# Queries and keys projected once per batch and copied into the row stacks by transfers of GpSimd

## The chip, the cores and the metric

The kernel runs on one core of a Trainium2 chip. Its engines are TensorE (PE in the profile; PEld is its weight load), VectorE (DVE), ScalarE (ACT), GpSimd (POOL) and SyncE (SP), beside 16 DMA engines. The metric is the device time of one execution in microseconds, as the median of several runs.

## The reference

The input is x of 16 batches, 512 rows, 128 columns, in f32. A layer norm gives xn, and the output is x plus an attention branch plus a feed-forward branch, both taken from xn:

```python
def attention(x, ...):                      # 16 heads of 8 columns
    xn = layernorm(x) * ln_g + ln_b
    q, k, v = xn @ Wq + bq, xn @ Wk + bk, xn @ Wv + bv
    p = pe @ Wp                              # sinusoidal positions
    content = einsum('bihd,bjhd->bhij', q + u_bias, k)
    pos = relative_shift(einsum('bihd,jhd->bhij', q + v_bias, p))
    attn = softmax((content + pos) * dh ** -0.5)
    return (attn @ v) @ Wo + bo

def feed_forward(x, ...):                    # weights are +1 or -1
    h = concatenate([x, -x])
    h = relu(s0 * h @ w0) * 2
    h = relu(s1 * h @ w1) * 2
    return s2 * h @ w2
```

`relative_shift` pads the 512x512 position scores of a head by a zero column and reads them back one element per row further on.

## The kernel before

**Units and halves.** A unit is one head of one batch: 256 units. The work runs in half steps ("halves"), two per unit and 32 per batch. In each half TensorE does, in this order: two position products and two content products of 128 query rows by 512 (lines 680, 690), eight 128x128 transposes of finished scores (line 699), one entry of a job table, and sixteen small products of transposed probabilities with values (line 713). The parts of a unit lie in different halves: its positions in halves 2u to 2u+3, its content scores twelve halves later, its transposes from half 2u+17.

**The way of the scores.** ScalarE copies the position scores of a half from PSUM into `pos_sb` (line 441). SyncE writes a unit's scores, 1026 KB, to a buffer `shift` in memory (line 285), and ScalarE's queue reads them back shifted by one element per row, 1024 KB, into `sc_sb` (line 428), issued in half 2u+8. VectorE then adds the content scores and takes the row minimum (line 574), subtracts it (line 582), and after the transposes ScalarE applies the exponential (line 451). So every unit moves 2050 KB, beside 256 KB of x and 256 KB of output per batch.

**Stacks.** For precision, queries, keys and positions are kept as a coarse part (f32r) and the remainder. A stack holds four heads, each in 32 partitions; of these, 26 rows are in use (`ROWS`): rows 0 to 7, 8 to 15 and 16 to 23 hold the eight columns of a head three times, and rows 24 and 25 carry the terms of the biases u and v. To bring them there, the weights themselves are laid out in this way (`stack_w`, loaded at the start), so that one projection of 128x512 in f32 makes one stack of one batch: the jobs `QG` (line 600) and `KG` (line 605), four groups of each per batch. ScalarE evicts each to `act_sb` with a bias (line 412), and GpSimd makes the stack in two operations of 128x512 (lines 338 and 339), in which a column `LOW_Q` or `LOW_K` of zeros and ones picks the rows that hold the remainder.

**Jobs.** The table (`EARLY` and `FRONT`, `MIDDLE`, `BACK` and `END`, lines 172 to 180) says in which half of which batch TensorE does which job: transposes of normalized rows (T1, TZ), the projections, the feed-forward layers L0, L1 and L2, values V, the outputs (TO, TH, WO, TY). It has 32 entries per batch, an L1 or L2 counting twice, so each of a batch's 32 halves has one. Most jobs are evicted by ScalarE and split by GpSimd (lines 347 and 348); jobs share three buffers in `act_sb` (`N_ACT`). GpSimd also computes the scales of the layer norm (lines 309 to 314) and the normalized rows (line 248), in the order of the halves.

**Start.** `EARLY` holds the first projections and the four position projections `PG`. The first query stack is made by VectorE (lines 488 and 489); until then no position product (line 680) can start. GpSimd sets three small tiles by memsets (lines 302 to 304) ahead of the first scales.

Of the kernel before, what the change touches and what calls it, by code (L numbers as in the profile page):

```python
# [5 lines left out]
ALU = mybir.AluOpType  # L6
# [8 lines left out]
ROWS = 26  # L15


def attention_mlp(nc, x, consts, stack_w, wp, pe_t, k0, k1, k2, out):
# [26 lines left out]
    with ExitStack() as ctx:  # L45
# [20 lines left out]
        w_sb = {n: const(D) for n in ("v", "o")}
        bias_q = const(GROUPS)
        bk_rows = const(GROUPS * DH).rearrange("p (g d) -> p g d", d=DH)
        uk_rows = const(GROUPS * DH).rearrange("p (g d) -> p g d", d=DH)
# [3 lines left out]
        stack_w_sb = sb("stack_w_sb", [P, 2, GROUPS * P])  # L73
        wq, wk = stack_w_sb[:, 0, :], stack_w_sb[:, 1, :]
        bias_k = sb("bias_k", [P, GROUPS])
        biased = sb("biased", [P, H, DH])
        by_bias = sb("by_bias", [P, 2, H])
        bk_uk = sb("bk_uk", [P, GROUPS, DH])
# [18 lines left out]
        KS = sb("k_stack", [P, GROUPS, S], F32R)  # L97
        PS = sb("p_stack", [P, GROUPS, S], F32R)
# [9 lines left out]
        o_t = sb("o_t", [P, S])  # L108
        wp_sb, pe_sb = o_t, heads[:, :, :, :].rearrange("p t h d -> p (t h d)")
# [7 lines left out]
        h2 = sb("h2", [P, C2, 2, S], F32R)  # L117
        y_t = sb("y_t", [P, S])
# [24 lines left out]
        s_qs, s_ks, s_ps = sem("s_qs"), sem("s_ks"), sem("s_ps")  # L143
# [28 lines left out]
        EARLY = ((-32, "TZ", 0), (-31, "PG", 0), (-30, "QG", 0), (0, "KG", 0), (1, "PG", 1), (1, "T1", 0),  # L172
                 (2, "QG", 1), (4, "PG", 2), (4, "L0", 0), (5, "L0", 1), (6, "KG", 1), (7, "PG", 3), (7, "L0", 2),
                 (8, "V", 0), (9, "QG", 2), (10, "KG", 2), (11, "L0", 3))
# [9 lines left out]
        STATS, NORM_X, NORM_Z = -50, -41, -27  # L184
# [12 lines left out]
        def job(name, b, c=0):  # L197
# [3 lines left out]
        BANK = {("TZ", 0, 0): ps_pt[:, 0, :], ("QG", 0, 0): ps_pt[:, 1, :], ("PG", 0, 0): ps_con[:, 0, :],  # L201
                ("PG", 0, 1): ps_con[:, 1, :], ("PG", 0, 2): ps_con[:, 0, :], ("PG", 0, 3): ps_con[:, 1, :],
                ("KG", 0, 0): ps_pt[:, 0, :]}
        RAW = {("QG", 0, 0): sc_sb[:, 4, 0, :], ("KG", 0, 0): sc_sb[:, 4, 1, :], ("PG", 0, 0): sc_sb[:, 5, 0, :],
               ("PG", 0, 1): sc_sb[:, 5, 1, :], ("PG", 0, 2): sc_sb[:, 5, 2, :], ("PG", 0, 3): sc_sb[:, 5, 3, :]}

        SPLITS = ("T1", "L0", "L1", "QG", "KG")
# [51 lines left out]
        def _(sp):  # L259
# [6 lines left out]
            sp.dma_start(stack_w_sb[:, :, :].rearrange("p a c -> p (a c)"), stack_w).then_inc(s_w, 16)  # L266
# [27 lines left out]
        def _(pool):  # L294
# [9 lines left out]
            pool.memset(v_sb[:, :, :, :, DH:DH + 1], 1.0).then_inc(s_ones, 1)  # L304

# [16 lines left out]
            def stack(dst, src, low, ready):  # L322
                own(pool.tensor_tensor(dst, src, low.broadcast_to([P, S]), ALU.mult))
                own(pool.tensor_tensor(dst, src, dst.bitcast(F32), ALU.subtract))
                pool.sem_inc(ready, 1)

            def split(name, b, c):
# [3 lines left out]
                if name in ("QG", "KG"):  # L331
                    dst, low, ready = {"QG": (QS, LOW_Q, s_qs), "KG": (KS, LOW_K, s_ks)}[name]
                    dst = dst[:, c, :]
                    if b == 0 and c == 1 and name == "QG":
                        pool.wait_ge(s_qs, 1)
                    if b > 0:
                        pool.wait_ge(s_con, scored(content_end(H * (b - 1) + GROUP * (c + 1) - 1), 2 * CONTENT_LAG))
                    own(pool.tensor_tensor(dst, src, low.broadcast_to([P, S]), ALU.mult))  # L338
                    pool.tensor_tensor(dst, src, dst.bitcast(F32), ALU.subtract).then_inc(s_hl, 1)  # L339
# [10 lines left out]

            scales(0)
            pool.wait_ge(s_c, 16)
            for h in HALVES:
                for name, b, c in taken(h):
                    if (name, b, c) == ("KG", 0, 0):
                        pool.wait_ge(s_jev, job("KG", 0))
                        stack(KS[:, 0, :], RAW[("KG", 0, 0)], LOW_K, s_ks)
                    elif (name, b, c) in ACTS:
                        split(name, b, c)
                if h == 5:  # L360
                    scales(1)
# [445 lines left out]
```

## Time and profile before

| | us |
|---|---|
| median of 3 runs | 1471.57 |
| range of the runs | 1469.15 to 1471.65 |
| the profiled execution | 1474.37 |
| its span in the profile | 1472.5 |

Busy times in the profiled execution: TensorE 1445.2 us (98%), VectorE 1332.8 us (91%), ScalarE 1228.7 us (83%), GpSimd 730.7 us (50%). The DMAs moved 550.40 MB at a mean of 374 GB/s.

How to read it: a busy share is an average over the whole span, and matmuls are pipelined with modelled ends, so times of single matmuls overlap. What a step costs TensorE is read from the start of one group to the start of the next. "DMA share" is the mean share of time in which the 16 DMA engines had a packet under way; it can lie a little above 1 where packets overlap. The windows and timelines count from the start of the span.

### The profile page before, as it was taken

The numbers are of one execution on the slowest core, as the hardware profiler recorded it, in microseconds if no ns is written. First come the engines' busy times: TensorE is split into PE (matmuls) and PEld (weight loads), VectorE is DVE, ScalarE is ACT, GpSimd is POOL, SyncE is SP. The second block draws the span as 40 slices with busy tenths as digits, with TensorE's granted clock in tenths as the row PEclk, the third lists the DMA queues.
The fourth block names the chain that finished last, engine by engine and source line by source line (L and its number), as shares of the span: only waits on it lengthen the run. The fifth ranks groups of instructions, "written<-read, shape, count | busy, mean of one in ns | idle before, by whom it ended". The sixth has DMA issues, their size and how long they took to land.

```text
span 1472.5 us, 41301 instructions
## 1 busy us (share of the span) xinstructions
PE 1445.2 (98%) x16040; PEld 955.1 (65%) x16040; DVE 1332.8 (91%) x3483; ACT 1228.7 (83%) x1368; POOL 730.7 (50%) x725
## 2 busy tenths in 40 slices
PE   6999999999999999999999999999999999999997
PEld 2466666666666666766666666666766666666664
DVE  4789999999989999999999999999999999989995
ACT  4588888888888888888888888888888888888873
POOL 4646555554554556455554555455455554534400
PEclk7699999999999999999999999999999999999998
DMA  3999999999999999999999999999999999999991
GB/s 131 346 377 401 384 392 397 385 399 374 402 390 372 403 384 401 376 399 392 380 402 383 391 389 392 392 382 396 386 394 392 382 406 376 401 377 390 393 402 41
DMA packets 80434, 550.40 MB, mean 374 GB/s; under 512 B 9328, under 2 KB 10096, under 8 KB 14704
## 3 DMA queue, kind: packets, MB, share of 16 engines
q1 hardware_dynamic: 42944, 278.35, 49.0%
q10 hardware_dynamic: 37296, 269.41, 47.4%
q8 instruction: 128, 2.10, 0.6%
q14 instruction: 66, 0.54, 0.1%
HBM read 274.57 MB, written 273.15 MB: 372 GB/s over the span
## 4 chain that ended last, share of the span: by engine, by line
PE 96%; ACT 2%; DVE 1%; DMA 0%; issue 0%; ACTq 0%; DVEq 0%
PE ps_pt L699 36%; PE ps_av L713 19%; PE ps_pos L680 14%; PE ps_job L641 12%; PE ps_job L605 4%; PE ps_job L600 4%; PE ps_job L620 2%; ACT pt_sb L451 1%; PE ps_job L616 1%; PE ps_job L611 1%; PE ps_job L628 1%; PE ps_con L690 1%; PE ps_con L608 1%; PE ps_job L624 1%; PE ps_job L622 0%; DMA heads<-in_pe_t 0%
## 5 line engine op out<-in xcount | busy, mean ns | idle before, releaser
L574 DVE CUSTOM_DVE_ANT_0 sc_sb<-ps_con,sc_sb 128x512 f32<-128x512 f32 x1024 | 663.0, 684 | 91.8 <-PE ps_con L690 90.5
L441 ACT COPY pos_sb<-ps_pos 128x1024 f32<-128x1024 f32 x510 | 518.4, 1017 | 184.5 <-PE ps_pos L680 183.8
L582 DVE TENSOR_SCALAR sc_sb<-sc_sb,nmax 128x512 f32<-128x512 f32 x1024 | 604.9, 623 | 0.1
L699 PE MATMUL ps_pt<-c_sb,sc_sb 128*128 128x128 f32 x4096 | 560.6, 280 | 3.9 <-ACT pt_sb L451 2.6
L451 ACT ACTIVATE pt_sb<-ps_pt 128x1024 f32<-128x1024 f32 x512 | 525.7, 1027 | 25.2 <-PE ps_pt L699 25.1
L699 PEld LDWEIGHTS ps_pt<-c_sb,sc_sb 128*128 128x128 f32 x4096 | 439.7, 141 | 130.5 <-issue 93.4
L713 PE MATMUL ps_av<-pt_sb,v_sb 128*9 128x128 f32 x8192 | 319.9, 274 | 0.6 <-ACT pt_sb L451 0.6
L713 PEld LDWEIGHTS ps_av<-pt_sb,v_sb 128*9 128x9 f32 x8192 | 172.8, 90 | 208.4 <-issue 205.7
L347 POOL CAST h<-act_sb 128x512 fp32r<-128x512 f32 x128 | 81.8, 639 | 397.3 <-ACT act_sb L417 397.0
L680 PE MATMUL ps_pos<-p_stack,q_stack 26*128 26x512 f32 x1024 | 262.5, 502 | 3.5 <-DVE q_stack L489 2.2
L690 PE MATMUL ps_con<-k_stack,q_stack 26*128 26x512 f32 x1024 | 262.1, 497 | 2.1 <-DVE nmax L574 2.0
L641 PE MATMUL ps_job<-h,w 128*128 128x512 f32 x640 | 190.6, 420 | 0.1
L680 PEld LDWEIGHTS ps_pos<-p_stack,q_stack 26*128 26x128 f32 x1024 | 98.1, 183 | 125.7 <-issue 115.6
L348 POOL TENSOR_TENSOR h<-act_sb,h 128x512 fp32r<-128x512 f32 x128 | 165.8, 1295 | 10.4
L338 POOL TENSOR_TENSOR k_stack<-act_sb,c_sb 128x512 fp32r<-128x512 f32 x63 | 71.1, 1129 | 115.9 <-ACT act_sb L412 115.7
L338 POOL TENSOR_TENSOR q_stack<-act_sb,c_sb 128x512 fp32r<-128x512 f32 x63 | 70.8, 1124 | 115.6 <-ACT act_sb L412 114.9
L641 PEld LDWEIGHTS ps_job<-h,w 128*128 128x128 f32 x640 | 109.7, 192 | 15.5 <-ACT act_sb L417 0.6
L690 PEld LDWEIGHTS ps_con<-k_stack,q_stack 26*128 26x128 f32 x1024 | 98.5, 182 | 6.5 <-DVE nmax L574 4.6
L417 ACT ACTIVATE act_sb<-ps_job,col 128x512 f32<-128x512 f32 x128 | 87.7, 685 | 1.5 <-PE ps_job L641 1.5
L339 POOL TENSOR_TENSOR q_stack<-act_sb,q_stack 128x512 fp32r<-128x512 f32 x63 | 80.7, 1281 | 4.9
L339 POOL TENSOR_TENSOR k_stack<-act_sb,k_stack 128x512 fp32r<-128x512 f32 x63 | 80.7, 1281 | 4.9
L574 DVE DVE_READ_ACCUMULATOR2_ANT nmax<- 128x1 f32 x1024 | 83.1, 81 | 0.0
(88 smaller groups left out, 941.3 us busy)
## 6 DMA issues: line engine op xcount, KB each, us to landing
shift<-pos_sb SPq DMA_DIRECT2D x256, 1026.0 KB, 9.0
sc_sb<-shift ACTq DMA_DIRECT2D x256, 1024.0 KB, 9.4
x_sb<-in_x SPq DMA_DIRECT2D x16, 256.0 KB, 11.0
out<-x_sb SPq DMA_DIRECT2D x16, 256.0 KB, 11.2
stack_w_sb<-in_stack_w SPq DMA_DIRECT2D x1, 512.0 KB, 5.1
c_sb<-in_consts ACTq DMA_DIRECT2D x1, 422.0 KB, 3.5
o_t<-in_wp ACTq DMA_DIRECT2D x1, 256.0 KB, 5.9
heads<-in_pe_t ACTq DMA_DIRECT2D x1, 256.0 KB, 6.7
```

The costliest lines, as they stand in the source:

```text
L338: own(pool.tensor_tensor(dst, src, low.broadcast_to([P, S]), ALU.mult))
L339: pool.tensor_tensor(dst, src, dst.bitcast(F32), ALU.subtract).then_inc(s_hl, 1)
L348: pool.tensor_tensor(dst[:, 1, :], src, dst[:, 0, :].bitcast(F32), ALU.subtract) \
L441: act.copy(to, ps_pos[:, :, :]).then_inc(s_pe, 1)
L451: act.activation(pt_sb[:, 2 * i:2 * i + 2, :], ps_pt[:, :, :], ACT.Exp, scale=-1.0) \
L574: dve.tensor_tensor_reduce(sc_sb[:, m % N_SC, t, :], ps_con[:, k, :], sc_sb[:, m % N_SC, t, :], -SCALE, 3.4e38, ALU.add, ALU.min, nmax[:, ...
L582: dve.tensor_scalar(sc_sb[:, m % N_SC, t, :], sc_sb[:, m % N_SC, t, :], nmax[:, m % N_SC, t:t + 1], None, ALU.subtract).then_inc(s_sub, 1)
L641: return pe.matmul(ps_job[:, :], lhs, src[:, a, hl, :], start=(a == 0 and hl == 0), stop=(a == len(before) - 1 and hl == 1))
L680: ins = pe.matmul(ps_pos[:, bank, :], QS[rows, g, t * P:(t + 1) * P], PS[rows, g, :], start=True, stop=True)
L690: pe.matmul(ps_con[:, bank, :], QS[rows, g, t * P:(t + 1) * P], KS[rows, g, :], start=True, stop=True).then_inc(s_con, 1)
L699: last = pe.transpose(ps_pt[:, j % 2, t * P:(t + 1) * P], sc_sb[:, u % N_SC, t, j * P:(j + 1) * P], id_sb)
L713: last = pe.matmul(ps_av[32 * t:32 * t + DH + 1, h % 4, :], v_sb[:, b % 2, j, h, :], pt_sb[:, j, t * P:(t + 1) * P], start=(j == 0), stop= ...
```

## The change

Queries and keys of a batch are projected once for all 16 heads, by jobs `QB` and `KB`: 128 output columns, with Wq and Wk as they are. ScalarE evicts each once, and GpSimd splits it into a coarse part and a remainder (`q_hl`, `k_hl`, 128 x 2 x 512). The stacks are then filled by transfers that GpSimd issues: a function `spread` copies, for one group of four heads, the 32 partitions of the group three times, into every fourth row of the stack from row 0, 1 and 2 (2 KB per row, 64 KB per transfer). For the queries these are coarse, coarse, remainder, for the keys coarse, remainder, coarse. That makes 24 transfers per batch: the queries of a group are issued in halves divisible by 8, eight halves before its first use, the keys in the halves after with remainder 2, ten halves before. Each group has a semaphore, and TensorE waits for 48 (three transfers of 16) per batch. GpSimd waits before each group until the content scores of that group in the batch before are done.

Row 3 of every four holds, for rows 3 and 7 of a head, the terms of the biases (`ROWS` is 32, `BIAS_ROWS` 3 and 7); the rest of the query stack is 1 and that of the key stack 0, set once by two memsets of 128x2048 on GpSimd at the start. The bias u is added to the queries (with bq), so the keys need no bias rows, and v - u takes the place of v for the positions.

The job table is laid out anew with 26 entries per batch. The stacked weights (512 KB) are no longer loaded; the constants grow by 190 columns. `o_t` now shares the memory of `z_sb`, for which GpSimd has one more wait before it normalizes z, and `wp_sb` that of `sc_sb`. The first query projection is split by VectorE, and GpSimd issues its transfers in half -8.

```diff
-ROWS = 26
+ROWS = 32
+BIAS_ROWS = (3, 7)
...
-        stack_w_sb = sb("stack_w_sb", [P, 2, GROUPS * P])
-        wq, wk = stack_w_sb[:, 0, :], stack_w_sb[:, 1, :]
...
+        q_hl = sb("q_hl", [P, 2, S], F32R)
+        k_hl = sb("k_hl", [P, 2, S], F32R)
...
-        FRONT = ((-16, "T1", 0), (-9, "TZ", 0), (-6, "V", 0), (-5, "QG", 0), (-3, "L0", 0), (-1, "KG", 0),
-                 (1, "KG", 1), (2, "QG", 1), (3, "L0", 1), (7, "L0", 2), (9, "QG", 2), (10, "KG", 2), (11, "L0", 3))
-        MIDDLE = ((12, "L1", 0, 2), (14, "KG", 3), (15, "QG", 3), (17, "L1", 1, 2), (20, "L1", 2, 2),
-                  (24, "L1", 3, 2), (36, "L2", 0, 2), (38, "TO", 0), (40, "TO", 1))
-        BACK = ((51, "TO", 2), (54, "TO", 3), (60, "TH", 0), (62, "WO", 0), (64, "TY", 0))
+        FRONT = ((-19, "T1", 0), (-18, "TZ", 0), (-11, "QB", 0), (-9, "V", 0), (-5, "L0", 0), (-3, "L0", 1),
+                 (-1, "KB", 0), (0, "L0", 2), (8, "L0", 3))
+        MIDDLE = ((9, "L1", 0, 2), (15, "L1", 1, 2), (17, "L1", 2, 2), (24, "L1", 3, 2), (33, "L2", 0, 2),
+                  (39, "TO", 0), (44, "TO", 1))
+        BACK = ((52, "TO", 2), (54, "TO", 3), (58, "TH", 0), (60, "WO", 0), (62, "TY", 0))
...
+            pool.memset(QS[:, :, :].bitcast(F32), 1.0).then_inc(s_fill, 1)
+            pool.memset(KS[:, :, :].bitcast(F32), 0.0).then_inc(s_fill, 1)
...
+                if k == 1:
+                    wait(pool, s_job, job("WO", b - 3))
...
-                if name in ("QG", "KG"):
-                    dst, low, ready = {"QG": (QS, LOW_Q, s_qs), "KG": (KS, LOW_K, s_ks)}[name]
-                    dst = dst[:, c, :]
...
-                    own(pool.tensor_tensor(dst, src, low.broadcast_to([P, S]), ALU.mult))
-                    pool.tensor_tensor(dst, src, dst.bitcast(F32), ALU.subtract).then_inc(s_hl, 1)
+                if name in ("QB", "KB"):
+                    dst, ready, landed = {"QB": (q_hl, s_qh, s_q), "KB": (k_hl, s_kh, s_k)}[name]
+                    wait(pool, landed[GROUPS - 1], 48 * b)
+                    own(pool.tensor_copy(dst[:, 0, :], src))
+                    pool.tensor_tensor(dst[:, 1, :], src, dst[:, 0, :].bitcast(F32), ALU.subtract).then_inc(s_hl, 1)
...
+            def spread(k, stack, hl, thirds, ready, landed):
+
+                b, g = divmod(k, GROUPS)
+                if not 0 <= b < B:
+                    return
+                pool.wait_ge(ready, b + 1)
+                if b > 0:
+                    pool.wait_ge(s_con, scored(content_end(H * (b - 1) + GROUP * (g + 1) - 1), 2 * CONTENT_LAG))
+                for third, part in enumerate(thirds):
+                    pool.dma_start(stack[third:P:4, g, :], hl[32 * g:32 * g + 32, part, :]).then_inc(landed[g], 16)
...
+                if h % 8 == 0:
+                    if h == -8:
+                        pool.wait_ge(s_fill, 2)
+                    spread(h // 8 + 1, QS, q_hl, (0, 0, 1), s_qh, s_q)
+                if h % 8 == 2:
+                    spread(h // 8, KS, k_hl, (0, 1, 0), s_kh, s_k)
...
-                if name == "QG":
-                    return [lambda: pe.matmul(out, wq[:, c * P:(c + 1) * P], z_q[:, :],
-                                              start=True, stop=True)]
+                if name == "QB":
+                    return [lambda: pe.matmul(out, w_sb["q"], z_q[:, :], start=True, stop=True)]
...
-                    pe.wait_ge(s_qs, GROUPS * b + g + 1)
+                    pe.wait_ge(s_q[g], 48 * (b + 1))
...
-                    pe.wait_ge(s_ks, GROUPS * b + g + 1)
+                    pe.wait_ge(s_k[g], 48 * (b + 1))
```

## Rows read from the trace of the kernel before

**Rows 1.** The page: busy engines; DMA queues (packets, MB, share); chain by engine.

```profile
PE 1445.2 (98%) x16040; PEld 955.1 (65%) x16040; DVE 1332.8 (91%) x3483; ACT 1228.7 (83%) x1368; POOL 730.7 (50%) x725
...
q1 hardware_dynamic: 42944, 278.35, 49.0%
q10 hardware_dynamic: 37296, 269.41, 47.4%
...
PE 96%; ACT 2%; DVE 1%; DMA 0%; issue 0%; ACTq 0%; DVEq 0%
```

**Rows 2.** Windows: length, busy us (instructions) per engine, PEclk, DMA share, GB/s.

```profile
105.00:700.00 595.00, 594.75 (x6783) 397.69 (x6776) 556.82 (x1460) 516.99 (x576) 318.91 (x315) 1.00 1.01 391
1405.00:1430.00 25.00, 24.32 (x305) 16.05 (x304) 23.73 (x68) 19.25 (x21) 1.90 (x2) 1.00 1.01 410
1412.00:1434.00 22.00, 21.54 (x259) 14.58 (x258) 20.34 (x58) 13.83 (x16) 0.00 (x0) 1.00 1.01 420
```

**Rows 3.** TensorE's timeline: start us, us, engine, line, operation, tiles.

```profile
617.04 1.06 PE L616 MATMUL ps_job<-c_sb,z_t 128*128 128x128 f32 x8
...
704.87 1.06 PE L616 MATMUL ps_job<-c_sb,z_t 128*128 128x128 f32 x8
...
707.77 1.02 PE L600 MATMUL ps_job<-z_q,stack_w_sb 128*128 128x512 f32 x2
708.73 0.62 PE L713 MATMUL ps_av<-pt_sb,v_sb 128*9 128x128 f32 x16
...
1418.19 0.50 PE L680 MATMUL ps_pos<-p_stack,q_stack 26*128 26x512 f32 x1
...
1420.20 0.49 PE L680 MATMUL ps_pos<-p_stack,q_stack 26*128 26x512 f32 x1
```

**Rows 4.** Waits: engine, line, releaser: total us, times, longest us.

```profile
DVE sc_sb L574 <- PE ps_con L690: 90.5, 147, 2.5
...
DVE stats L480 <- DMA x_sb<-in_x: 2.2, 1, 2.2
```

**Rows 5.** DMA: landing (page); then 2.5 to 9 us; then 25 to 36.5 us.

```profile
shift<-pos_sb SPq DMA_DIRECT2D x256, 1026.0 KB, 9.0
...
DMA packets 2043, 2.28 MB, mean 350 GB/s; under 512 B 610, under 2 KB 1360, under 8 KB 2043
...
q1 hardware_dynamic: 304, 2.23, 46.9%
...
shift<-pos_sb SPq DMA_DIRECT2D x3, 1026.0 KB, 4.7
```

**Rows 6.** Groups: engine, operation, tiles, count | busy us, mean ns | idle before.

```profile
L582 DVE TENSOR_SCALAR sc_sb<-sc_sb,nmax 128x512 f32<-128x512 f32 x1024 | 604.9, 623 | 0.1
...
L347 POOL CAST h<-act_sb 128x512 fp32r<-128x512 f32 x128 | 81.8, 639 | 397.3 <-ACT act_sb L417 397.0 <-DVE v_sb L497 0.2 <-POOL k_stack L339 0.2
...
L339 POOL TENSOR_TENSOR q_stack<-act_sb,q_stack 128x512 fp32r<-128x512 f32 x63 | 80.7, 1281 | 4.9
...
L338 POOL TENSOR_TENSOR k_stack<-act_sb,c_sb 128x512 fp32r<-128x512 f32 x63 | 71.1, 1129 | 115.9 <-ACT act_sb L412 115.7 <-POOL rstd L314 0.2
```

**Rows 7.** Timeline, VectorE and GpSimd together; then L582 from 1410 us (min/median/max ns).

```profile
710.78 1.28 POOL L339 TENSOR_TENSOR q_stack<-act_sb,q_stack 128x512 fp32r<-128x512 f32 x1
...
711.05 1.29 DVE L582 TENSOR_SCALAR sc_sb<-sc_sb,nmax 128x512 f32<-128x512 f32 x1
...
L582 DVE TENSOR_SCALAR sc_sb<-sc_sb,nmax x20: 477/482/485, 1410.3 to 1431.8; 128x512 f32<-128x512 f32 x20
```

**Rows 8.** Timeline of the start.

```profile
0.80 0.33 POOL L304 MEMSET v_sb<- 128x128 f32 x1
...
5.00 0.19 POOL L309 TENSOR_SCALAR var_eps<-mv 128x4 f32<-128x4 f32 x1 [3.88 <-DVE mv L484]
...
16.14 0.50 PE L680 MATMUL ps_pos<-p_stack,q_stack 26*128 26x512 f32 x1 [2.23 <-DVE q_stack L489]
...
31.19 2.04 PE L605 MATMUL ps_job<-z_t,stack_w_sb 128*128 128x512 f32 x2
```

More of the change, by code:

```diff
@@ L14, with attention_mlp @@
 GROUP = 4
-ROWS = 26
-def attention_mlp(nc, x, consts, stack_w, wp, pe_t, k0, k1, k2, out):
+ROWS = 32
+BIAS_ROWS = (3, 7)
+def attention_mlp(nc, x, consts, wp, pe_t, k0, k1, k2, out):
     B, S, D = x.shape
@@ L62, in attention_mlp @@
         id_sb = const(P)
-        cols = const(8)
-        G, BB, BO, S0, S1, S2, LOW_Q, LOW_K = (cols[:, i:i + 1] for i in range(8))
+        cols = const(10)
+        G, BB, BO, S0, S1, S2, BQ, BK, U, LOW_K = (cols[:, i:i + 1] for i in range(10))
         bv_row = const(D)
[L66 to L69, printed above, removed]
+        w_sb = {n: const(D) for n in ("q", "k", "v", "o")}
         u_all = const(D).rearrange("p (h d) -> p h d", d=DH)
@@ L142, in attention_mlp @@
         s_hl = sem("s_hl")
-        s_qs, s_ks, s_ps = sem("s_qs"), sem("s_ks"), sem("s_ps")
+        s_fill = sem("s_fill")
+        s_qh, s_kh = sem("s_qh"), sem("s_kh")
+        s_q = [sem(f"s_q{g}") for g in range(GROUPS)]
+        s_k = [sem(f"s_k{g}") for g in range(GROUPS)]
+        s_ps = sem("s_ps")
         s_pos, s_con = sem("s_pos"), sem("s_con")
@@ L354, in _ @@
                 for name, b, c in taken(h):
[L355 to L358, printed above, removed]
+                    if (name, b, c) in ACTS:
                         split(name, b, c)
+                if h % 8 == 0:
[4 more added lines that the diff above has]
+                    spread(h // 8, KS, k_hl, (0, 1, 0), s_kh, s_k)
                 if h == 5:
@@ L519, in _ @@
             dve.wait_ge(s_c, 16)
-            dve.wait_ge(s_w, 48)
+            dve.wait_ge(s_w, 32)
             def heads_first(w):
                 return w.rearrange("p (h r) -> p h r", r=32)
-            for i, (w, by) in enumerate(((wp_sb[:, :], v_all), (wk, u_all))):
-                own(dve.tensor_tensor(biased[:, :, :], heads_first(w)[:, :, 0:DH], by, ALU.mult))
-                own(dve.reduce_sum(by_bias[:, i, :], biased[:, :, :], axis=mybir.AxisListType.X))
-                for r in (ROWS - 2, ROWS - 1):
-                    last = dve.tensor_copy(heads_first(w)[:, :, r], by_bias[:, i, :])
-                last.then_inc(s_bias, 1)
-            own(dve.tensor_tensor(bk_uk[:, :, :], bk_rows, uk_rows, ALU.mult))
-            dve.reduce_sum(bias_k[:, :], bk_uk[:, :, :], axis=mybir.AxisListType.X).then_inc(s_bias, 1)
+            w = heads_first(wp_sb)
+            own(dve.tensor_tensor(v_all, v_all, u_all, ALU.subtract))
+            own(dve.tensor_tensor(biased[:, :, :], w[:, :, 0:4 * DH:4], v_all, ALU.mult))
+            own(dve.reduce_sum(by_bias[:, :], biased[:, :, :], axis=mybir.AxisListType.X))
+            for r in BIAS_ROWS:
+                last = dve.tensor_copy(w[:, :, r], by_bias[:, :])
+            last.then_inc(s_bias, 1)
+            dve.tensor_tensor(bias_q[:, :], BQ, U, ALU.add).then_inc(s_bias, 1)
             dve.tensor_scalar(col2[:, 0:2], cols[:, 3:5], 2.0, None, ALU.mult).then_inc(s_bias, 1)
@@ L540, in _ @@
             stack(PS[:, 0, :], RAW[("PG", 0, 0)], LOW_K, s_ps)
-            dve.wait_ge(s_jev, job("QG", 0, 0))
-            stack(QS[:, 0, :], RAW[("QG", 0, 0)], LOW_Q, s_qs)
+            dve.wait_ge(s_jev, job("QB", 0))
+            own(dve.tensor_copy(q_hl[:, 0, :], RAW[("QB", 0, 0)]))
+            dve.tensor_tensor(q_hl[:, 1, :], RAW[("QB", 0, 0)], q_hl[:, 0, :].bitcast(F32), ALU.subtract) \
+               .then_inc(s_qh, 1)
             dve.wait_ge(s_rstd, 2)
@@ L653, in do_job @@
                 if part == 0 and (name, b, c) in BANK:
-                    if name in ("QG", "PG") and c == 0:
-                        pe.wait_ge(s_w, 48)
+                    if name == "PG" and c == 0:
+                        pe.wait_ge(s_w, 32)
                     if name == "PG":
```

104 lines of the change are left out of this document (35 added, 69 removed).

## The prediction

> **What bounds the kernel now.** I read the page first: TensorE is busy for 98% of the span and makes up 96% of the chain that ended last, VectorE is at 91%, and the two large DMA queues together fill 49.0 + 47.4 = 96.4% of the 16 DMA engines [rows 1]. So TensorE looks like the bound, with a second resource that has almost nothing left. The windows say it for the steady part: from 105 to 700 us TensorE is busy 594.75 of 595 us, and the DMA share is 1.01 at 391 GB/s [rows 2]. TensorE's timeline gives the period: the job of line 616 comes once per batch, at 617.04 and at 704.87 us, so a batch takes 87.83 us [rows 3]. Who waits for whom shows that the DMAs are full but not yet late: VectorE's large wait (90.5 us) is for TensorE's content scores, and the only wait for a transfer in the list is 2.2 us for x at the start [rows 4]. But a write of 1026 KB takes 9.0 us to land in the middle of the run and 4.7 us when it runs nearly alone [rows 5]: transfers queue up behind each other.
>
> **What goes from TensorE.** Each batch has four query and four key projections of 128x512 in f32. One of them occupies TensorE from 707.77 to 708.73 us, 0.96 us [rows 3]. The change keeps one of each, so six go: 6 x 0.96 = 5.8 us per batch, 92 us in all. The job table has 32 entries per batch in 32 halves now and 26 afterwards, so six halves are left with no job. Near the end a half without one takes from 1418.19 to 1420.20, 2.01 us [rows 3], only 0.73 us less than the mean half of 87.83/32 = 2.74 us, since other engines then come last. So six jobs save between 6 x 0.73 = 4.4 and 5.8 us on the path; I take the middle, 5.2. If nothing else intervened, a batch would take 87.83 - 5.2 = 82.6 us.
>
> **VectorE and GpSimd.** VectorE is busy 556.82/595 x 87.83 = 82.2 us per batch [rows 2], so it too could only just follow. Part of this is not its own work. Its line 582 lasts 623 ns on average [rows 6], but 482 ns late in the run, where GpSimd does nothing, and 1.29 us where it lies over GpSimd's line 339 [rows 7]: 64 x 0.14 = 9 us per batch are waiting for GpSimd. GpSimd is busy 318.91/595 x 87.83 = 47.1 us per batch. The change takes eight splits of 1.129 + 1.281 us from it (-19.3) and adds two of 0.639 + 1.281 (+3.8) [rows 6], which leaves 31.6, and with it a third less collision: VectorE falls to about 79 us. Against this GpSimd now issues 24 transfers per batch. The trace has no transfer issued by GpSimd, so I bound one by its smallest and its large operations, 0.33 us [rows 8] and 1.28 us [rows 6], and take the middle, 0.8: 19 us, which brings GpSimd to 51 us and VectorE back to about 83. Nothing urgent stands behind the issues: query stacks are issued 8 halves ahead of use (8 x 2.74 = 22 us), key stacks 10, and even queued transfers land in 9.0 us [rows 5]. ScalarE loses six evictions, which lie beside other work. All of this is near 83 us per batch, still 5 us below today.
>
> The Trainium skill (SBUF — State Buffer, "SBUF: two separate sides") says that a DMA issued by GpSimd waits for its descriptors while VectorE holds the port they share. The trace shows that lock in the other direction only [rows 7]. By the page a spread could come late by about one line 582 each time; with 22 us in hand that changes no term here.
>
> **The DMA engines.** Here I see the end of the gain. A batch now moves 391 GB/s x 87.83 us = 34.3 MB. The change adds 24 copies of 32 rows of 2 KB, 1.57 MB, from SBUF to SBUF. For 82.6 us this asks for 35.9/82.6 = 434 GB/s. The best that the trace shows over 22 us is 420, over 25 us 410 [rows 2]; writes that run alone move 2.23 MB in 0.469 x 11.5 us, 413 GB/s [rows 5]. So the DMA engines become the bound whatever the other engines save. What a batch costs then is uncertain on two counts. First the rate for the large transfers: between 391 (today's, if full engines can't do better) and 420. I take 410, the rate of the longer stretch, since it also holds some of the ordinary jobs. 34.3/410 = 83.7 us. Second the price of the copies: at 420 GB/s 3.7 us; at the 350 GB/s of the setup, where all packets are small [rows 5], 4.5 us. I take 4.5, as these packets are small. Sum: 88.2 us per batch against 87.83, so +0.4 us, and over 15 periods +6 us. The ends are 34.3/420 + 3.7 = 85.4 us (-36 us in all) and 34.3/391 + 4.5 = 92.2 us (+66 us).
>
> **The start.** The first stack of queries now comes by transfer: three issues and a landing stand between the split and line 680, which starts at 16.14 us today [rows 8]. Below, 1.5 us; above, three issues of 1.28 and the 4.7 us of a lone large write, 8.5; I take 4.5, because a copy is a sixteenth of that write. Two memsets of 2048 elements now stand ahead of the scales on GpSimd. By line 304 (0.33 us for 128 elements) they cost 5.3 us each, by line 347 (0.639 us for 512) 2.6 each; GpSimd is free from 1.13 to 5.00 us [rows 8], so the delay lies between 1.2 and 6.7 us, and I take 1.5, since a memset reads nothing. Four projections leave the first twelve halves, where one lasts 2.04 us [rows 8]: between 0 and 8.2 us, and I take 4, for much of the waiting there is for evictions and splits. Setup loads 512 KB of stacked weights less and 95 KB of constants more, 1.2 us at 350 GB/s. Sum 4.5 + 1.5 - 4 - 1 = +1 us, between -7 and +14.
>
> **The sum.** Span 1472.5 + 6 + 1 = 1479.5 us. The profiled execution took 1474.37 us, 1.9 more than its span and 2.8 more than the median of the runs, 1471.57. So I expect 1479.5 + 1.9 - 2.8 = 1478.6, about 1479 us.
>
> **The rivals.**
> *The engines pace it (B).* 82.6 to 83 us per batch; 16 x 5 = 80 us less, about 1392 us. For it speaks that TensorE is the whole chain [rows 1] and no wait is for a DMA [rows 4]. It needs 434 GB/s held through, which no stretch of the trace shows. The Trainium skill (DMA: Bandwidth & Descriptors, "Specifications") gives 435 GB/s as the fabric's ceiling; by that page the rival would be just possible.
> *Memory, not the DMA engines, sets 391 GB/s (C).* Then copies that never leave SBUF slip into the engines' stretched packets and cost nothing, and a batch stays at 34.3/391 = 87.8 us: 1473 us. Against it stand 420 GB/s of almost only memory traffic late in the run [rows 2]. The Trainium skill (DMA: Bandwidth & Descriptors, "Bandwidth") says that the memory side binds such transfers at about 358 GB/s and the fabric the SBUF copies; the trace's 391 is above its figure.
> *The copies cost twice (D), the slower side.* They are read from 32 neighbouring partitions and written to rows four apart, so a copy's engine crosses partitions that other transfers are using at that moment. If each holds an engine for its reading and its writing in turn, a batch costs 83.7 + 9.0 = 92.7 us: 15 x 4.9 + 1 = +74 us, about 1546. It decides the sign as soon as a copy's packets take over 4.1/4.5 = 0.9 of what I charged, at 410 GB/s.
> *Forecast (A).* The DMA engines bound it, 85.4 to 92.2 us per batch.
>
> **Chances.** A 0.70 (faster 0.26, within 0.2% 0.10, slower 0.34: its centre lies 7 us above today and its spread is some 30), B 0.10, C 0.08 (0.06 within, 0.02 faster by a good start), D 0.12. So faster 0.38, same 0.16, slower 0.46; 0.2%, 3 us, is about what a measurement of this kernel can tell from no change. The range reaches A's lower end with the start's middle (1479 - 42) and most of the way to its upper one (1479 + 60), and leaves out B and most of D: 1436 to 1530 us.
>
> **What the profile would show.** A: a batch period near 88 us, a DMA share of 1.0 or more at 400 GB/s or above, waits of VectorE or ScalarE for shift transfers that the trace has none of now, write landings well above 9.0 us, and TensorE busy near 93%. TensorE's step: no more than two pairs of line 600/605 matmuls per batch. GpSimd: about 50 us per batch and line 582's mean between 0.55 and 0.65 us. B would show a period below 84 us at 430 GB/s. C: a share of 1 at 391 GB/s plus the copies. D: the queue of the copies taking over 6 us of 16 engines per batch. I would be wrong above all if full engines do clearly better than 420 GB/s, or if copies of 2 KB rows cost far from 4.5 us.

## The result, and the profile after

The changed kernel takes 1502.29 us (median of 4 runs, 1495.67 to 1506.52) against 1471.61 us for the kernel before in the same series (1469.15 to 1473.47): a ratio of 1.0205, 95% interval 1.0163 to 1.0248. It is 31 us slower. The profiled execution took 1495.67 us, its span is 1493.8 us, 21.3 us more than the span before.

The page of the changed kernel: busy engines, the three large queues (packets, MB, share of the 16 DMA engines' time), the chain by engine and by line.

```profile
PE 1384.0 (93%) x15848; PEld 940.0 (63%) x15848; DVE 1289.7 (86%) x3479; ACT 1169.9 (78%) x1272; POOL 683.3 (46%) x919
...
q1 hardware_dynamic: 42800, 277.83, 47.4%
q10 hardware_dynamic: 37296, 269.51, 44.5%
...
q0 software_dynamic: 18432, 25.19, 5.7%
...
PE 65%; DMA 22%; ACT 6%; issue 2%; DVE 2%; ACTq 1%; POOL 1%; POOLq 0%
```

Against [rows 1]: TensorE has lost 61 us of work and is idle 7% of the span; DMA, which had no part of the chain, now makes up 22% of it. Queue 0, which is new, holds the copies. The two large queues move the same bytes as before (within 0.1%) and take 91.9% of 1493.8 us instead of 96.4% of 1472.5 us: 1373 us instead of 1419. Packets took less time each although more was moved per microsecond. More on this at the end.

Windows of the changed kernel (length, busy us and instructions of PE, PEld, DVE, ACT and POOL, granted clock, DMA share, GB/s): the long one, and four that follow each other.

```profile
105.00:700.00 595.00, 558.14 (x6557) 383.32 (x6556) 528.36 (x1426) 481.51 (x525) 285.63 (x383) 0.99 1.02 400
726.00:737.00 11.00, 11.00 (x129) 7.39 (x128) 11.00 (x26) 9.35 (x11) 7.06 (x9) 1.00 1.01 415
737.00:748.00 11.00, 10.54 (x142) 7.06 (x140) 10.55 (x31) 10.18 (x11) 5.45 (x8) 1.00 1.04 412
748.00:759.00 11.00, 7.48 (x76) 5.63 (x73) 7.60 (x21) 5.98 (x8) 1.63 (x2) 0.88 1.02 417
759.00:770.00 11.00, 10.87 (x128) 7.67 (x126) 9.11 (x25) 8.62 (x10) 5.37 (x9) 0.97 1.01 371
```

The rate is 400 GB/s over the long window, where it was 391 [rows 2]. TensorE is not short of work evenly: it works through two windows and then stands still for 3.5 us of 11, while the DMA engines move 417 GB/s. The timeline of that stop, ScalarE and TensorE:

```profile
748.28 1.02 ACT L446 COPY pos_sb<-ps_pos 128x1024 f32<-128x1024 f32 x1
...
754.08 0.52 ACTq L433 DMA_DIRECT2D sc_sb<-shift  x1
...
754.70 1.01 ACT L446 COPY pos_sb<-ps_pos 128x1024 f32<-128x1024 f32 x1 [4.14 <-DMA shift<-pos_sb]
...
755.76 0.49 PE L682 MATMUL ps_pos<-p_stack,q_stack 32*128 32x512 f32 x1 [2.79 <-ACT pos_sb L446]
```

ScalarE waits until a write of position scores has landed. Only then can it issue the read of them (L433) and copy new scores into the buffer (L446), and only then has TensorE somewhere to put the next product. The list of waits counts such stops, with the new waits for transfers; then what transfers take to land:

```profile
DVE sc_sb L581 <- PE ps_con L692: 124.6, 162, 4.2
...
ACT pos_sb L446 <- DMA shift<-pos_sb: 80.6, 30, 4.5
...
DVE sc_sb L581 <- DMA sc_sb<-shift: 6.7, 13, 2.0
...
PE ps_pos L682 <- DMA q_stack<-q_hl: 6.1, 1, 6.1
```

```profile
shift<-pos_sb SPq DMA_DIRECT2D x256, 1026.0 KB, 11.0
sc_sb<-shift ACTq DMA_DIRECT2D x256, 1024.0 KB, 11.0
q_stack<-q_hl POOLq DMA_DIRECT2D x192, 64.0 KB, 7.5
k_stack<-k_hl POOLq DMA_DIRECT2D x192, 64.0 KB, 7.6
```

[Rows 4] had one wait for x and none for the shift; writes landed in 9.0 us [rows 5]. TensorE waits for a stack once in the whole run, for the very first.

The batch period comes from the output projection, one pair of matmuls per batch some 0.45 us apart. Its first and last start in the first 14 batches (minimum, median and maximum ns of one; first to last start), in the kernel before and then in the changed one:

```profile
L611 PE MATMUL ps_job<-o_t,c_sb x28: 592/594/595, 188.3 to 1331.2; 128*128 128x512 f32 x28
```

```profile
L616 PE MATMUL ps_job<-z_sb,c_sb x28: 592/594/595, 183.9 to 1345.9; 128*128 128x512 f32 x28
```

13 periods take 1142.4 us before and 1161.5 after: 87.9 and 89.35 us, 1.47 more. Over 15 periods that is 22.0 us, so everything else together, start and end, gave back 0.7 us. The question is therefore why a batch takes 89.4 us. (The median run takes 6.6 us longer than the profiled one; if that lies in the 15 periods, its batch takes 89.8.)

### The profile page after: what moved, and what is told of

Same layout as the page of the kernel before. It is cut to its first block, busy times and chain, and to the rows that moved or that the text cites. A ratio compares the mean times of both kernels' runs of the same rounds, so it can differ in the third digit from the quotient of the medians.

```text
span 1493.8 us, 40812 instructions
## 1 busy us (share of the span) xinstructions
PE 1384.0 (93%) x15848; PEld 940.0 (63%) x15848; DVE 1289.7 (86%) x3479; ACT 1169.9 (78%) x1272; POOL 683.3 (46%) x919
## 4 chain that ended last, share of the span: by engine, by line
PE 65%; DMA 22%; ACT 6%; issue 2%; DVE 2%; ACTq 1%; POOL 1%; POOLq 0%
PE ps_pt L701 26%; DMA shift<-pos_sb 21%; PE ps_av L715 12%; PE ps_job L646 11%; PE ps_pos L682 10%; ACT pt_sb L456 4%; ACT pos_sb L446 2%; PE ps_job L625 1%; PE ps_job L616 1%; PE ps_job L611 1%; ACTq L433 1%; PE ps_job L621 1%; PE ps_job L607 1%; DMA sc_sb<-shift 1%; DVE sc_sb L581 1%
## 5 line engine op out<-in xcount | busy, mean ns | idle before, releaser
L446 ACT COPY pos_sb<-ps_pos 128x1024 f32<-128x1024 f32 x510 | 519.0, 1018 | 241.8 <-PE ps_pos L682 155.2
L589 DVE TENSOR_SCALAR sc_sb<-sc_sb,nmax 128x512 f32<-128x512 f32 x1024 | 555.8, 575 | 0.1
L682 PE MATMUL ps_pos<-p_stack,q_stack 32*128 32x512 f32 x1024 | 263.6, 505 | 58.1 <-ACT pos_sb L446 51.5
L692 PE MATMUL ps_con<-k_stack,q_stack 32*128 32x512 f32 x1024 | 262.6, 501 | 0.0
L682 PEld LDWEIGHTS ps_pos<-p_stack,q_stack 32*128 32x128 f32 x1024 | 98.5, 185 | 180.0 <-issue 106.7
L646 PE MATMUL ps_job<-h,w 128*128 128x512 f32 x640 | 201.9, 440 | 0.0
L354 POOL DMA_DIRECT2D q_stack<-q_hl x192 | 107.5, 562 | 8.0 <-DVE q_hl L548 6.8
L354 POOL DMA_DIRECT2D k_stack<-k_hl x192 | 102.5, 536 | 4.4 <-issue 4.4
L692 PEld LDWEIGHTS ps_con<-k_stack,q_stack 32*128 32x128 f32 x1024 | 98.5, 183 | 2.7 <-issue 1.3
L574 DVE COPY o_sb<-ps_av 128x512 f32<-128x512 f32 x64 | 43.9, 686 | 28.3 <-PE ps_av L715 27.3
L646 PE MATMUL ps_job<-x_t,w 128*128 128x512 f32 x128 | 47.2, 449 | 3.8 <-DVE v_sb L502 2.6
```

Source lines behind the costliest of these rows:

```text
L354: pool.dma_start(stack[third:P:4, g, :], hl[32 * g:32 * g + 32, part, :]).then_inc(landed[g], 16)
L446: act.copy(to, ps_pos[:, :, :]).then_inc(s_pe, 1)
L589: dve.tensor_scalar(sc_sb[:, m % N_SC, t, :], sc_sb[:, m % N_SC, t, :], nmax[:, m % N_SC, t:t + 1], None, ALU.subtract).then_inc(s_sub, 1)
L646: return pe.matmul(ps_job[:, :], lhs, src[:, a, hl, :], start=(a == 0 and hl == 0), stop=(a == len(before) - 1 and hl == 1))
L682: ins = pe.matmul(ps_pos[:, bank, :], QS[rows, g, t * P:(t + 1) * P], PS[rows, g, :], start=True, stop=True)
L692: pe.matmul(ps_con[:, bank, :], QS[rows, g, t * P:(t + 1) * P], KS[rows, g, :], start=True, stop=True).then_inc(s_con, 1)
```

## The experiments

Times are medians; ratios are against the kernel before on the same chip (1471.5 to 1472.9 us).

**Which engines pace the two kernels.** Two runs, one of each kernel, leave out half of every write and every read back from the seventh head on:

```diff
-sp.dma_start(chunks(shift[u % N_SHIFT]), pos_sb[:, u % N_POS]...)
+part = 1 if u < N_SHIFT else 2
+sp.dma_start(chunks(shift[u % N_SHIFT, 0:S * PITCH // part]), pos_sb[:, u % N_POS]...[:, 0:NT * PITCH // part])
```

and the read back in the same way. On the changed kernel:

> The changed kernel with all of its copies, but from the seventh head on each position write and each read back moves only half of its bytes. Left out: half of the position scores. T1: the DMA engines fall to about half and the engines set the pace: by the prediction's step 82.6 us per batch, so about 1392 to 1400 us, with TensorE near 99%. If TensorE or VectorE had a price of the change that the prediction missed (stalls for stacks that land late, GpSimd's port), the time stays above 1420 us, and the waits name it.

Measured: 1413.75 us, ratio 0.9596 (0.9581 to 0.9610). On the kernel before:

> The kernel before, with each position write and each read back from the seventh head on halved. Left out: half of the position scores. It gives the pace of the engines of before without the DMA engines. The changed kernel so halved had a period of 83.9 us, the same in every batch. Theory T1 (before is paced by its engines, the changed kernel by its transfers): the period stays at 87.8 us and the time at 1471 us (1466 to 1474). Rival T4 (both are paced by the DMA engines, whose share reads 1.01 in both): it falls to 84 us or below, 1420 us or less.

Measured: 1471.30 us, ratio 0.9994 (0.9984 to 1.0004). The windows and the output projection of both, first the changed kernel with half the transfers, then the kernel before with half:

```profile
105.00:1300.00 1195.00, 1181.33 (x14114) 813.01 (x14106) 1126.43 (x3054) 1039.53 (x1126) 607.25 (x814) 1.00 0.72 227
...
L618 PE MATMUL ps_job<-z_sb,c_sb x28: 592/594/595, 180.0 to 1271.4; 128*128 128x512 f32 x28
```

```profile
105.00:1300.00 1195.00, 1194.79 (x13628) 798.41 (x13625) 1117.34 (x2920) 1038.42 (x1158) 636.70 (x627) 1.00 0.59 199
...
L613 PE MATMUL ps_job<-o_t,c_sb x28: 592/594/595, 186.2 to 1328.4; 128*128 128x512 f32 x28
```

The kernel before has the same period with half the transfers, (1328.4 - 0.5 - 186.2)/13 = 87.8 us: its engines pace it, and the DMA share of 1.01 that it showed [rows 2] cost it nothing that this measurement can tell (the interval allows 2.4 us). The changed kernel's engines need (1271.4 - 0.5 - 180.0)/13 = 83.9 us. That is more than the 82.6 of the prediction, and the time lies between the two that the expectation had set apart (1400 and 1420). So the change does what it says: some 57 us of 1471 less for the engines (1413.75 against 1471.30). The transfers take all of it back, and 31 us more.

**What the copies cost.** Three runs: the changed kernel without copies from batch 1 on, the same with the query copies only, and the kernel before with 24 copies per batch added to it:

```diff
-if not 0 <= b < B:
+if b != 0:                                      # no copies
+if not 0 <= b < B or (b > 0 and stack is KS):   # queries only
```

> The changed kernel, but GpSimd copies queries and keys into the stacks only for batch 0; all later batches multiply with the stacks of batch 0. Left out: the filling of the stacks from batch 1 on, so the scores of batches 1 to 15 are not the reference's. Theory T1 (the DMA engines' time is the bound, and the 24 copies per batch took 5.3 us of it): the period falls from 89.3 us to about 84 us, the whole to about 1502 - 15 x 5.3 = 1420 us (1405 to 1435), DMA share still 1.0 or near it. Rival T2 (memory alone sets the rate of the large transfers, the copies slip in free, and the time was lost elsewhere, by TensorE's clock or by later evictions): 1490 to 1500 us. Rival T3 (the copies cost more than their packets show, since they hold up the large ones): below 1400 us, the engines' own pace of about 82.6 us.

Measured: 1459.99 us, ratio 0.9902 (0.9877 to 0.9926).

> The changed kernel with the query copies in every batch and the key copies in batch 0 only: 12 copies per batch instead of 24. Left out: the filling of the key stacks from batch 1 on. T1: the saving is linear in the copies, half of that without any, so about 1460 us (1450 to 1470). T2: 1490 to 1500 us. T3: the same line with a steeper slope. A threshold (all of the gain or none of it at half the dose) would show as a time off the middle between this kernel's neighbours.

Measured: 1486.52 us, ratio 1.0084 (1.0058 to 1.0111).

> The kernel before, all of its eight projections and its arithmetic kept, with 24 copies of 64 KB per batch added by GpSimd into a scratch tile that nobody reads. T1: 34.3 MB of large transfers at about 400 GB/s take 85.8 us and the copies 5.3, so the period rises from 87.83 to about 91 us and the whole from 1471.6 to about 1520 us (1500 to 1550); the 2 us between TensorE's 87.8 and the DMA engines' own 85.8 absorb a part. T2: no change, 1472 to 1476. T3: above 1550. If the issuing on GpSimd is what costs (VectorE held off the port), line 582 and its like get longer than their mean of 623 ns here, and the DMA queues do not.

Measured: 1513.61 us, ratio 1.0258 (1.0227 to 1.0289). Here the added lines are

```diff
+for third, part in enumerate(thirds):
+    pool.dma_start(twin[third:P:4, :], stack_w_sb[32 * g:32 * g + 32, part, :]).then_inc(s_twin[j], 16)
```

24 copies cost 42 us in the changed kernel (2.8 per batch) and 41 in the kernel before (2.7); 12 cost 27. So they aren't free (T2 falls), and no run came near the times of T3, which wanted more than the packets show. But the first expectation was missed by 40 us: the run without any copies should have come to 1420 and stayed at 1460, far above the engines' 1414. Half of the explanation was wrong: the large transfers alone need more than I had thought. The second expectation, 1450 to 1470 for half of the copies, was missed with it. Nor is the price even: the first twelve copies cost 27 us and the next twelve 16. Why is open.

Is it GpSimd's issuing that costs, by holding up VectorE? In the changed kernel it isn't: VectorE's subtraction lasts 575 ns with the copies and 572 without. In the kernel before the added copies lengthen it from 623 to 639 ns, 64 x 0.016 = 1 us per batch, so there a part of the 41 us may be of this kind.

**What the large transfers need by themselves.** TensorE's work is cut down, once without the copies from batch 1 on and once with all of them. Both runs leave out the products of the low parts in the layers L0, L1 and L2, 24 matmuls per batch:

```diff
-return [lambda a=a, hl=hl: product(a, hl) for a in range(len(before)) for hl in range(2)]
+return [lambda a=a: product(a, 0) for a in range(len(before))]
```

> The changed kernel without the copies from batch 1 on (as in the run without copies, 1460 us, a period of 86.5 us), and without the products of the low parts in L0, L1 and L2. Left out: the filling of the stacks from batch 1 on, and the low halves of the split products. TensorE has 24 matmuls of 0.43 us less per batch, 10 us. It asks whether 86.5 us is what the large transfers need by themselves. Theory T1 with 397 GB/s as the most that the DMA engines can hold in this mix: 86.5 us again, 1455 to 1462. Rival T6 (they can hold 410 to 420, as the forecast had it, and 86.5 is a near tie of engines at 83.9 and transfers at 82 to 84, in which each waits for the other now and then): 83 to 84 us, 1415 to 1430.

The 10 us in this and the next expectation are too much: matmuls overlap, so their lengths don't add up. From start to start a job of four matmuls takes 1.10 us and one of two 0.65 (the changed kernel, then the one with 24 matmuls less):

```profile
737.22 1.17 PE L646 MATMUL ps_job<-h,w 128*128 128x512 f32 x4
738.32 0.63 PE L715 MATMUL ps_av<-pt_sb,v_sb 128*9 128x128 f32 x16
```

```profile
735.95 0.72 PE L646 MATMUL ps_job<-h,w 128*128 128x512 f32 x2
736.60 0.63 PE L715 MATMUL ps_av<-pt_sb,v_sb 128*9 128x128 f32 x16
```

That is 0.23 us for a matmul and some 5.5 us for a batch, of the order of the change's own step.

Without copies and low products, measured: 1443.28 us, ratio 0.9817 (0.9782 to 0.9852).

> The changed kernel with all of its copies, without the products of the low parts in L0, L1 and L2: TensorE has 24 matmuls less per batch, 10 us. Left out: the low halves of the split products. It answers the run that had neither these products nor the copies (1443 us). Theory T1 (the changed kernel is bound by its transfers, TensorE's work hardly counts): 1485 to 1500 us, and the copies cost 1492 - 1443 = 49 us or 3.3 us per batch here, where the engines are well out of the way. Rival T6 (much of the 1502 is a tie of engines and transfers, which wait for each other by turns): 1460 to 1475, and the copies' own price is 1 to 2 us per batch.

Measured: 1503.38 us, ratio 1.0219 (1.0193 to 1.0244), beside the changed kernel once more:

> The changed kernel once more, unedited, as the mark for its variants: the moved jobs gave 1506 us and the plain copies 1511, and the first measurement of the changed kernel 1502. 1498 to 1508 us; above 1508 the two edits would be no slower than it.

Measured: 1502.73 us, ratio 1.0204 (1.0181 to 1.0227). Its waits of ScalarE for writes, and those of the run with the copies and without the low products:

```profile
ACT pos_sb L446 <- DMA shift<-pos_sb: 80.5, 33, 4.5
```

```profile
ACT pos_sb L446 <- DMA shift<-pos_sb: 154.5, 95, 4.6
```

The run without copies lies between its two forecasts (1455 to 1462 and 1415 to 1430); the one with them lies 3 us above T1's range and 28 above T6's, so T6 falls. With the copies, 5.5 us less of TensorE per batch change nothing (+0.7 us in all); the time turns into waits for writes. So the changed kernel is bound by its transfers, and TensorE's work no longer counts. Without the copies the same step is worth 16.7 us in all, 1.1 per batch. My reading is that engines (83.9) and transfers are close there, and each holds up the other now and then; it rests on the medians alone, since the profiled executions of the two happen to be the fastest of one and the slowest of the other (1453.8 and 1453.1 us). With less work for the engines the 24 copies cost 1503.38 - 1443.28 = 60 us, 4.0 us per batch.

The period of the run without copies and low products is what the large transfers need by themselves, at most; then that of the changed kernel in its repeated run (span 1500.5 us):

```profile
L614 PE MATMUL ps_job<-z_sb,c_sb x28: 592/594/595, 178.9 to 1306.4; 128*128 128x512 f32 x28
```

```profile
L616 PE MATMUL ps_job<-z_sb,c_sb x28: 592/594/595, 186.2 to 1353.0; 128*128 128x512 f32 x28
```

The first is (1306.4 - 0.5 - 178.9)/13 = 86.7 us in an execution 9.8 us longer than the median, which makes 86.0 us in the median run (an estimate: 86.7 - 9.8/15). The second is (1353.0 - 0.5 - 186.2)/13 = 89.7 us, and 89.7 less the 4.0 of the copies gives 85.7. So the large transfers alone need some 86 us. Both figures are about one rate: 34.3 MB in 86 us are 399 GB/s, and 35.9 MB in 89.7 us are 400. The windows from 105 to 700 us say it directly, in this order: no copies; no copies and less TensorE; copies and less TensorE; the kernel before with the copies.

```profile
105.00:700.00 595.00, 575.39 (x6825) 394.92 (x6824) 546.15 (x1483) 500.44 (x544) 213.23 (x234) 0.99 1.01 398
```

```profile
105.00:700.00 595.00, 556.75 (x6695) 376.77 (x6693) 558.43 (x1490) 494.46 (x548) 213.14 (x235) 0.99 1.01 400
```

```profile
105.00:700.00 595.00, 538.04 (x6418) 364.37 (x6417) 538.86 (x1428) 472.99 (x525) 287.71 (x384) 0.98 1.03 401
```

```profile
105.00:700.00 595.00, 584.17 (x6579) 388.41 (x6576) 550.36 (x1411) 500.54 (x562) 393.84 (x461) 0.99 1.01 397
```

397 to 401 GB/s in these, with copies and without. Over all runs that wait for writes and in both long windows (105 to 700 and 105 to 1300 us) it is 393 to 401; the lowest are the two with 12 copies per batch, 393 to 395. A copy costs about its bytes at that rate: 1.57 MB/400 = 3.9 us per batch.

What sets this rate is open. The writes use four buffers (`N_POS`), and no run has another number of them. Two things speak against too few transfers in flight: the copies come on a queue of their own, on top of the others, and the sum doesn't rise with them; and in the run with the copies and without the low products the share stays at 0.99 or above in every stretch of 5.5 us from 704 to 880 us.

**Whether it matters how a copy is made.** One run reads the same rows that it writes, one names both sides f32:

```diff
-pool.dma_start(stack[third:P:4, g, :], hl[32 * g:32 * g + 32, part, :])
+pool.dma_start(stack[third:P:4, g, :], hl[third:P:4, part, :])
+pool.dma_start(stack[third:P:4, g, :].bitcast(F32), hl[32 * g:32 * g + 32, part, :].bitcast(F32))
```

> The changed kernel, with each copy read from the same rows that it writes (third, third + 4, ...), not from 32 neighbouring ones. Left out: the right content of the stacks. The prediction's rival D had it that a copy that crosses partitions costs twice. Theory T8 (crossing from one set of partitions to another is part of the price): the packets of the copies get shorter than 98 ns and the time falls by half of the copies' 42 us, to about 1480. Rival (a copy costs its bytes and packets, wherever its rows lie): 1498 to 1508 us and 5.7% of the engines' time.

Measured: 1503.53 us, ratio 1.0207 (1.0175 to 1.0239).

> The changed kernel, output unchanged, with both sides of the copies named f32, not float32r, in the same order on GpSimd. A copy packet of 2 KB takes 98 ns in the trace, a packet of x of the same size 84. Theory T7 (a copy between tiles of float32r is handled as a cast, and that makes its packets slower): packets fall to some 84 ns, 5.7% of the engines' time to 4.9%, and the time by 24 x 32 x 14 ns / 16 = 0.7 us per batch, 10 us. Rival: a float32r copy is a plain copy; 1498 to 1505 and 5.7% again.

Measured: 1510.99 us, ratio 1.0268 (1.0251 to 1.0285). Queue 0 (packets, MB, share) of the two, in the same order:

```profile
q0 software_dynamic: 18432, 25.19, 5.5%
```

```profile
q0 software_dynamic: 12288, 25.19, 4.7%
```

Crossing partitions costs nothing that shows (1503.5 against 1502.7 us), so T8 falls. The f32 copies take a third fewer packets for the same bytes (32 per copy instead of 48) and 4.7% of the engines' time instead of 5.5 to 5.7%, near the 4.9% of T7, and the kernel isn't faster for it; it is even 0.6% slower than the changed kernel (the intervals 1.0251 to 1.0285 and 1.0181 to 1.0227 don't touch). Why it is slower stays open. What follows is that the sum of packet times isn't the price.

**Whether the order of work costs something.**

```diff
-(33, "L2", 0, 2), (39, "TO", 0)
+(35, "L2", 0, 2), (38, "TO", 0)
```

> The changed kernel, output unchanged, with two jobs moved: L2 from halves 33 and 34 to 35 and 36, the first TO from 39 to 38. The six halves without a job are then 1, 2, 5, 7, 11 and 19 of each batch instead of 3, 4, 5, 6, 11 and 19. In the trace of the changed kernel TensorE stops for 3.5 to 4 us once per batch (748 to 759 us and 836 to 847 us), just behind the four empty halves in a row, and in the 11 us after it the DMA engines move 371 to 374 GB/s instead of 401 to 420. Theory T5 (uneven work lets the engines outrun the transfers, stop, and leave the transfers short afterwards): that costs up to (410 - 372)/410 x 11 = 1 us per batch, so the time falls by 8 to 15 us to about 1490. Rival T1 pure (the DMA engines need the same time whatever the order): 1498 to 1505, no difference over 3 us, and a stop of the same sum elsewhere.

Measured: 1506.09 us, ratio 1.0237 (1.0215 to 1.0259): no gain, T5 falls. The stops move, they don't go: ScalarE's waits for writes sum to 72.9 us instead of 80.5,

```profile
ACT pos_sb L446 <- DMA shift<-pos_sb: 72.9, 30, 4.8
```

and the window from 770 to 781 us now has 350 GB/s. The low rate behind a stop is no loss that this levelling won back: over the long windows the mean is 397 to 399, against 399 to 401 without it.

**Half of the change.** Queries projected once and copied, keys projected per group as before:

```diff
-(0, "KB", 0) ... (-1, "KB", 0)
+(0, "KG", 0), (3, "KG", 1), (11, "KG", 2), (19, "KG", 3)
```

> Half of the change, output unchanged: queries projected once and copied (12 copies per batch), keys projected per group as before, into rows four apart. T1: the transfers of the run with half of the copies (1486 us) and 2.9 us more of TensorE per batch, which lies beside them: 1486 to 1495 us, no gain over the kernel before. If the engines' pace counted for more than the transfers, 29 jobs per batch at 85.9 us would come close to it: 1475 or below. It would beat both kernels only below 1470.

Measured: 1494.61 us, ratio 1.0150 (1.0102 to 1.0198). The fourth key projection lies at half 19, behind the refilling of `z_t` for the next batch at half 14, so the keys of its group come from the wrong batch; the amount of work is the same. It is slower than the kernel before, and than the same copies without the three projections (1486.5). There is little room for any dose of this change: without a single copy, which no version can have, it ends at 1460 us, 13 us below the kernel before, and twelve copies cost twice that (27 us). Doses below twelve weren't run.

## Why the prediction was right, and where it was not

The time, 1502 against the forecast 1479, lies in the range, and the mechanism is the forecast one: the transfers become the bound and take back what the engines save. But the range is wide, 94 us with both signs in it, faster had a chance of 0.38, and of the 31 us measured only 7 were forecast: the mechanism was foreseen, the size was not. Its terms, one by one:

- **The bound of before** [rows 1 to 4]: TensorE, with the transfers full but not late. Shown by the halved transfers (87.8 us per batch and 1471.3 us again).
- **TensorE's step.** 5.2 us per batch were taken, from 4.4 to 5.8. The engines' pace fell from 87.8 to 83.9, by 3.9: below the lower bound. TensorE's work did go by 87.8 - 1181.33/1195 x 83.9 = 4.9 us; but it is then idle 1 us per batch, mostly for VectorE and ScalarE. Even so, the term doesn't reach the sum, since the transfers are later.
- **VectorE and GpSimd.** VectorE is busy 1126.43/1195 x 83.9 = 79.1 us per batch in the run with half transfers, forecast 83. GpSimd is busy 42.6 us, forecast 51: a copy's issue takes 0.54 to 0.56 us, not 0.8. VectorE's L589 lasts 575 ns (0.55 to 0.65 forecast):

```profile
L589 DVE TENSOR_SCALAR sc_sb<-sc_sb,nmax 128x512 f32<-128x512 f32 x1024 | 555.8, 575 | 0.1
...
L354 POOL DMA_DIRECT2D q_stack<-q_hl x192 | 107.5, 562 | 8.0 <-DVE q_hl L548 6.8
L354 POOL DMA_DIRECT2D k_stack<-k_hl x192 | 102.5, 536 | 4.4 <-issue 4.4
```

- **The rate of the large transfers: the term that was mis-sized.** I took 410 GB/s from a 25 us window late in the run, "the rate of the longer stretch, since it also holds some of the ordinary jobs". Over 595 us the changed kernel has 400 GB/s, and the kernels that wait for their transfers have 393 to 401: some 86 us instead of 83.7. Windows of 11 us range from 371 to 420 in one batch of the changed kernel (704 to 792 us), so a window much shorter than a batch can't give a sustained rate; and 391 of the kernel before was not a limit either, but what its engines asked for. The value lay between my two bounds, and I took it near the wrong one.
- **The copies.** 4.5 us were charged, at 350 GB/s; they cost 4.0 us where transfers bind most clearly, their bytes at 400. The charge for small packets wasn't needed. It hid a part of the miss: the two errors have opposite signs.
- **Sum.** 83.7 + 4.5 = 88.2 was forecast, and the period measured is 89.7, of which some 86 are the large transfers' and 4 the copies'. 1.5 us x 15 = 22 us, which is the miss of 23.
- **The start** was forecast at +1 us. Start and end together come to -0.7. The first position product starts 19.04 - 16.14 = 2.9 us later [rows 8], where 4.5 were charged for the first stack by transfer and 1.5 for the memsets. These took 1.9 us each, in GpSimd's idle time: the first scales wait for VectorE, not for them.

```profile
0.97 1.87 POOL L304 MEMSET q_stack<- 128x2048 f32 x1
2.78 1.81 POOL L305 MEMSET k_stack<- 128x2048 f32 x1
5.92 0.19 POOL L310 TENSOR_SCALAR var_eps<-mv 128x4 f32<-128x4 f32 x1 [1.34 <-DVE mv L489]
...
15.64 1.86 POOL L354 DMA_DIRECT2D q_stack<-q_hl  x3 [6.75 <-DVE q_hl L548]
...
19.04 0.79 PE L682 MATMUL ps_pos<-p_stack,q_stack 32*128 32x512 f32 x1 [6.08 <-DMA q_stack<-q_hl]
```

- **The rivals.** B (the engines pace it, 1392) is what halving the transfers shows, 1414; it would have needed 34.3 + 1.6 = 35.9 MB in 83.9 us, 428 GB/s held, and 401 is what holds. C (memory sets the rate, copies that stay in SBUF are free) falls: they cost their full bytes, 60 us, so transfers to memory and those inside SBUF share what limits the rate, whatever it is. D (a copy costs twice, for crossing) falls: same rows, same time.
- **In the profile**: a period near 88 (89.4 to 89.7), a share over 1 at 400 GB/s or above (1.02, 400), waits for shift transfers (80.6 us), landings well above 9.0 (11.0) and TensorE at 93% (93%) all came.

The Trainium skill (Perfetto Trace Analysis, "Identifying the Most-Contended Engine") says not to judge the DMA by the busy share of its engines, which misleads, but by the use of the memory's bandwidth. The halved run of the kernel before agrees: half the bytes, and a share of 0.59 where 1.01 stood before.
The Trainium skill (DMA: Bandwidth & Descriptors, "Bandwidth") measures 425 GB/s for one core with a 16 MB transfer; with 1 MB transfers in both directions no kernel here held more than 401 over 595 us or longer.

## What to carry to other kernels

When one engine is at 98% and the DMA engines are full, find out which of the two is binding before taking work from the engine: halve the transfers and look whether the period moves. Then cost the new transfers by their bytes at the sustained rate of a stretch of several periods, never at that of a favourable window. Here the two were 2% apart (87.8 and some 86 us), and a change that took 57 us from the engines and added 4.6% to the bytes lost.

## What the runs showed of the hardware

- **A busy share of the DMA engines is no measure of how much room is left.** Half the large transfers gave a share of 0.59 (kernel before, 199 GB/s) and 0.72 with the copies (227 GB/s); the full kernel before read 1.01, and halving its transfers changed its time by 0.8 us (1472.1 to 1471.3). Packets took longer where nothing waited for them: those of the two large queues took 1419 us in the kernel before and 1373 in the changed one, which waits for them, for the same bytes.
- **The sustained rate was nearly the same, 393 to 401 GB/s, for all mixes that waited for writes**, with 0, 12 or 24 copies of 64 KB per batch, TensorE at 90 to 98%. Neither the number of packets per copy (32 or 48) nor its partitions moved it out of that band.
- **Two bounds near each other can cost more than the larger.** Engines at 83.9 and transfers at some 86 took about 1 us per batch more than with less work for TensorE. In the kernel before with the copies, engines at 87.8 and transfers at 89.7 gave 87.8 + 2.7 = 90.5, 0.8 over the larger, but there VectorE's work had grown by 1 us too. Engines at 87.8 and transfers at some 86 (the kernel before) gave nothing. That the two hold each other up in turns is my reading; no run shows it by itself.
- **TensorE's granted clock fell behind its stop.** In the changed kernel it stood nearly still from 754 to 756 us; the granted clock is 1.00 in that stretch, 0.58 and 0.57 in the two after it, near the lower level of 1.2 GHz, and 1.00 again from 760 us. A job of four matmuls took 1.73 us from start to start there (758.37 to 760.10) where it takes 1.10 otherwise. Since 5.5 us less of TensorE's work per batch didn't change the time, I take it that this costs nothing here.

```profile
754.00:756.00 2.00, 0.24 (x4) 0.19 (x4) 0.00 (x0) 1.30 (x2) 0.00 (x0) 1.00 1.02 419
756.00:758.00 2.00, 1.49 (x10) 1.25 (x7) 1.70 (x5) 2.00 (x3) 0.63 (x2) 0.58 1.01 404
758.00:760.00 2.00, 2.00 (x8) 1.51 (x6) 1.59 (x2) 1.14 (x2) 2.00 (x3) 0.57 1.03 392
760.00:762.00 2.00, 2.00 (x30) 1.44 (x29) 1.21 (x2) 0.77 (x1) 0.93 (x2) 1.00 0.99 404
```
